# A backward row transform in 64x64 tiles of TensorE, with the halves combined on VectorE

## The chip, the cores and the metric

The kernel runs on one core of one Trainium2 chip. The metric is the device time of one execution in microseconds (us); the median of three executions before the change is 3488.26 us, from 3488.07 to 3488.36. The engines are named PE (TensorE matmul), PEld (TensorE weight load), DVE (VectorE), ACT (ScalarE), POOL (GpSimd) and SP (SyncE, which issues most DMAs).

## The reference

Four layers act on an image batch of 4 x 64 channels x 128 x 128 in fp32: a box convolution, an AFNO block stack, and two more box convolutions. The change touches the AFNO stack alone, and in it only the inverse transform. Cut to what matters, one of its four blocks computes, for each of the four images:

```python
xf = jnp.fft.rfft2(_ln(xp, ln1w, ln1b), axes=(1, 2), norm='ortho')
# ... two 64x64 complex channel mixes (relu, then a threshold mask) per frequency
xs = jnp.fft.irfft2(xc, s=(H, W), axes=(1, 2), norm='ortho')
x = residual + jnp.transpose(xs, (0, 3, 1, 2))
h = jax.nn.gelu(_ln(xp2) @ mw1 + mb1, approximate=False)
x = x + jnp.transpose(h @ mw2 + mb2, (0, 3, 1, 2))
```

irfft2 is done as matrix products: first along the row frequencies (the part that is changed, called backward in the kernel), then along the column frequencies (called inverse).

## The kernel before, in words

Function `afno_layers` works through 16 runs (4 images x 4 blocks), numbered n. A run takes 16 steps q, a step takes 4 slots s. In every step each engine does one sixteenth of the MLP of run n (transpose in, up product, gelu, down product, transpose back, residual add). In between, in the slots, it does parts of the Fourier path of run n+1: forward transform, spectrum (the channel mixes), backward, and the first inverse parts. There is no scheduler: each engine's program is written out in this order, `parts_before` and the constants `U_...` tell which parts fall into which slot, and semaphores tie the engines together. Each engine takes its instructions in order.

Backward stands in step 11, slots 44 to 47. Before the change it is 16 parts, four in a slot. A part is four channels: PE multiplies the masked spectrum of each channel (128 row frequencies x 128) by the matrix `dft_hi` (128 x 128) into one PSUM bank (line 1756), and one copy brings the bank into `iy`, which shares the memory of `g`; VectorE copies the even parts (L1431), ScalarE the odd ones (L1568). Four banks are used in turn, so a part waits only for the copy of the part four earlier. fp32 products appear in the trace as two weight loads and two matmuls each.

Step 11 is one of the steps in the list `CLOSED`: PE does the two transposes (L1792 back, L1786 in), then all of backward without a break, and then the MLP products: up (L1766), down (L1777), up (L1766). Step 12 then begins with inverse part 0 (L1687 to L1691), which waits until all of `iy` is there. In step 11 VectorE also does the residual add (L1437) and two sums over a strip of the image (`sum_up`: L1456 sums the strip, L1459 sums its squares, which ScalarE makes at L1610). In three of the sixteen backward sections (where `fresh(n)` holds and another image is to come) ScalarE also fills a strip of a stage (`fill_stage`, L1621) between the second and the third slot of step 11.

```python
parts(n, q, 0, inverse, forward, spectrum, backward)    # slot 0 of a step
late = (2 if q in CLOSED else 3) if q == 5 or q % 4 == 3 and fresh(n) else 1
```

Of the kernel before, what the change touches and what calls it, by code (L numbers as in the profile page):

```python
# [32 lines left out]
P = 128  # L33
# [27 lines left out]

def constants():
# [10 lines left out]
    out[DFT_HI] = np.cos(turn)  # L73
    out[DFT_HI][:, HALF + 1:] = np.sin(turn[:, HALF + 1:])
# [12 lines left out]
    mirror = np.eye(P)[-n % P]  # L87
    out[SYM_E], out[SYM_O] = (np.eye(P) + mirror) / 2, (np.eye(P) - mirror) / 2
# [798 lines left out]
U_INVERSE, U_FORWARD, U_SPECTRUM, U_BACKWARD, U_NEXT, U_END = 0, 4, 20, 39, 55, 59  # L887
# [7 lines left out]
def parts_before(slot):  # L895
# [7 lines left out]
    if slot <= NEXT_SLOTS[0]:  # L903
        return U_BACKWARD + 4 * (slot - BACKWARD_SLOT)
# [105 lines left out]
def afno_layers(nc, const, w, src, dst, kept, early, s_early, s_early_par, s_last):  # L1010
# [6 lines left out]
    with ExitStack() as ctx:  # L1017
# [14 lines left out]
        bank = [psum(f"bank{i}") for i in range(4)]  # L1032
# [14 lines left out]
        iy = g[:].rearrange("p k r c -> p (k r c)")[:, 0:C * P].rearrange("p (h c) -> p h c", c=C)  # L1047
# [41 lines left out]
        s_ih, s_iy = sem("ih"), [sem("iy_dve"), sem("iy_act")]  # L1089
# [14 lines left out]
        def o1_of(j):  # L1104

            return odd[:].rearrange("p h c -> p (h c)") if j % 2 else o1[:]

# [48 lines left out]
        with nc.Block() as block:  # L1156
# [185 lines left out]
            def _(dve):  # L1342
# [132 lines left out]
                for n, q in periods():  # L1475
# [6 lines left out]
                    if q in CLOSED and 0 <= Q - 2 < BLOCKS * RUNS:  # L1482
                        residual(Q - 2)
                    parts(n, q, 0, inverse, forward, spectrum, backward)
# [15 lines left out]
                    strips = strips_at(n, q)[:1]  # L1500
                    late = (2 if q in CLOSED else 3) if q == 5 or q % 4 == 3 and fresh(n) else 1
                    for s in range(1, 4):
# [4 lines left out]
                        if s == late:  # L1507
# [4 lines left out]
                        if s == late + 1 and q in CLOSED:  # L1512
# [9 lines left out]
            def _(act):  # L1522
# [143 lines left out]
            def _(pe):  # L1666
# [11 lines left out]
                def inverse(n, j):  # L1678
                    if j == 0:
                        pe.wait_ge(s_iy[0], GROUPS // 2 * (n + 1))  # L1680
                        pe.wait_ge(s_iy[1], GROUPS // 2 * (n + 1))
# [67 lines left out]
                def backward(n, i):  # L1749
# [3 lines left out]
                    if i >= 4:  # L1753
# [132 lines left out]
```

## Time and profile before

| what | value |
|---|---|
| median of three executions | 3488.26 us |
| the profiled execution's own time | 3488.49 us |
| its span, first to last instruction | 3486.2 us |
| PE busy | 3236.5 us, 93% |
| DVE / ACT / POOL busy | 2363.6 / 2197.1 / 1689.7 us |
| mean granted TensorE clock | 0.962 |
| PE, backward matmuls (L1756) | 235.7 us busy, 2048 instructions |
| DVE, copies of backward (L1431) | 88.5 us, 128 instructions |
| ACT, copies of backward (L1568) | 76.0 us, 128 instructions |

The time outside the span is 2.3 us. A matmul's end is modelled, and matmuls are pipelined, so the distance from one start to the next says more than a duration. The granted clock is given as a share of 2.4 GHz, whose two levels here are 2.4 and 1.2 GHz.

### The profile page before, as it was taken

What the parts mean: (1) busy time and instruction counts of PE and PEld (TensorE: products, weight loads), DVE (VectorE), ACT (ScalarE), POOL (GpSimd) and SP (SyncE); (2) the same over time, 40 slices, a digit from 0 to 9 for tenths busy, and PEclk for the clock granted to TensorE, in tenths of its full rate; (3) what the DMA queues carried; (4) which work ended last, traced back from release to release, by engine and by line L of the source; (5) the groups of instructions that cost most, each with busy time, mean ns of one, the idle gap of its engine ahead of it and who ended that gap; (6) DMA issues with size and microseconds to landing.
All of it is one profiled execution on the core that took longest, in us unless ns stands there. A gap on an engine that the chain in (4) does not pass through costs nothing. (4 is left out here: it accounts for less than half of the span.)

```text
span 3486.2 us, 52802 instructions
## 1 busy us (share of the span) xinstructions
PE 3236.5 (93%) x18285; PEld 1963.5 (56%) x18285; DVE 2363.6 (68%) x4046; ACT 2197.1 (63%) x3477; POOL 1689.7 (48%) x1421
## 2 busy tenths in 40 slices
PE   6945699999999999999999999999999999979689
PEld 2735465657565656464646565757565656344257
DVE  4956667777777676766666767676767675536667
ACT  3955566666666666767676666575757575646468
POOL 4435546464646455555464655545454643310242
PEclk7967899999999999999999999999999999989789
DMA  9860001010202111313120111111111111457898
GB/s 328 274 200 19 37 31 66 32 67 31 67 31 67 37 66 39 120 43 142 50 88 37 65 41 61 43 55 43 55 43 55 43 55 43 169 178 204 273 292 241
DMA packets 250280, 334.10 MB, mean 96 GB/s; under 512 B 22304, under 2 KB 195616, under 8 KB 242608
## 3 DMA queue, kind: packets, MB, share of 16 engines
q1 hardware_dynamic: 241664, 315.29, 26.8%
q0 software_dynamic: 7904, 15.57, 1.6%
q8 instruction: 145, 2.38, 0.3%
q14 instruction: 103, 0.84, 0.1%
q10 hardware_dynamic: 464, 0.02, 0.0%
HBM read 188.06 MB, written 142.74 MB: 95 GB/s over the span
## 5 line engine op out<-in xcount | busy, mean ns | idle before, releaser
L1576 ACT ACTIVATE images<-a_wide,a_up_b 128x1024 f32<-128x1024 f32 x512 | 569.8, 1113 | 253.0 <-PE a_wide L1766 249.7
L1766 PE MATMUL a_wide<-images 64*128 64x512 f32 x2048 | 579.0, 641 | 26.6 <-ACT images L1576 25.9
L1318 POOL TENSOR_TENSOR images<-a_o,a_mag 128x256 f32<-128x256 f32 (+1 forms) x512 | 360.4, 730 | 371.6 <-DVE a_mag L1426 368.8
L1276 POOL TENSOR_TENSOR images<-images,a_stat 128x512 f32<-128x512 f32 x256 | 267.2, 1044 | 544.6 <-DVEq L1473 528.1
L1777 PE MATMUL a_result<-images 128*64 128x512 f32 x2048 | 495.9, 605 | 1.8 <-DVE images L1437 1.8
L1406 DVE TENSOR_TENSOR a_o<-a_bank,a_mix_b 128x512 f32<-128x512 f32 (+1 forms) x272 | 180.9, 665 | 248.7 <-PE a_bank L1723 241.8
L1739 PEld LDWEIGHTS a_bank<-a_dft_h,a_g 128*128 128x128 f32 x2080 | 272.4, 191 | 129.0 <-issue 129.0
L1766 PEld LDWEIGHTS a_wide<-images 64*128 64x128 f32 x2048 | 156.6, 185 | 289.2 <-issue 259.4
L1437 DVE TENSOR_TENSOR images<-a_result,images 128x512 f32<-128x512 f32 x256 | 175.7, 686 | 205.6 <-PE a_result L1792 205.2
L1777 PEld LDWEIGHTS a_result<-images 128*64 128x64 f32 x2048 | 124.4, 136 | 322.4 <-issue 318.8
L1459 DVE TENSOR_REDUCE a_stat<-a_sq 128x16 f32<-128x1024 f32 x240 | 290.7, 1211 | 22.1 <-ACT a_sq L1610 20.4
L1705 PE MATMUL a_bank<-dft_w,images 128*128 128x128 f32 x2048 | 246.1, 279 | 46.5 <-POOL images L1301 45.2
L1716 PE MATMUL a_bank<-a_xf,a_mix_fold 128*128 128x512 f32 (+1 forms) x544 | 283.2, 602 | 6.0 <-ACT a_xf L1563 6.0
L1456 DVE TENSOR_REDUCE a_stat<-images 128x16 f32<-128x1024 f32 x232 | 281.4, 1213 | 7.2 <-DVE a_stat L1005 0.5
L1705 PEld LDWEIGHTS a_bank<-dft_w,images 128*128 128x128 f32 x2048 | 235.6, 193 | 81.9 <-POOL images L1301 45.3
L1589 ACT ACTIVATE images<-a_result,a_down_b 128x512 f32<-128x512 f32 x256 | 175.5, 685 | 166.5 <-PE a_result L1777 166.5
L1739 PE MATMUL a_bank<-a_dft_h,a_g 128*128 128x128 f32 x2080 | 277.3, 275 | 1.8 <-DVE a_g L1399 1.8
L1610 ACT ACTIVATE a_sq<-images 128x1024 f32<-128x1024 f32 x216 | 226.8, 1050 | 26.1 <-DVE a_stat L1459 25.2
L1756 PE MATMUL a_bank<-a_dft_hi,images 128*128 128x128 f32 x2048 | 235.7, 278 | 5.2 <-POOL images L1318 5.2
L1756 PEld LDWEIGHTS a_bank<-a_dft_hi,images 128*128 128x128 f32 x2048 | 232.7, 194 | 8.6 <-POOL images L1318 8.6
L1264 POOL TENSOR_TENSOR images<-images,a_odd 128x512 f32<-128x512 f32 (+1 forms) x128 | 160.9, 1257 | 103.3 <-DVE images L1373 101.5
L420 ACT ACTIVATE box_pre<-box_bank,box_affine_k 128x128 f32<-128x128 f32 x512 | 192.2, 457 | 26.9 <-PE box_bank L484 25.1
(206 smaller groups left out, 6109.9 us busy)
## 6 DMA issues: line engine op xcount, KB each, us to landing
rows<-images SPq DMA_DIRECT2D x112, 512.0 KB, 2.6
images<-rows SPq DMA_DIRECT2D x105, 512.0 KB, 3.7
box_xc<-in_x SPq DMA_DIRECT2D x16, 1024.0 KB, 16.5
box_x<-in_x SPq DMA_DIRECT2D x64, 256.0 KB, 4.5
turned<-box_o SPq DMA_DIRECT2D x64, 256.0 KB, 3.6
images<-turned SPq DMA_DIRECT2D x16, 1024.0 KB, 13.0
planes<-box_work SPq DMA_DIRECT2D x64, 256.0 KB, 3.5
box_xc<-planes SPq DMA_DIRECT2D x16, 1024.0 KB, 18.8
```

The lines of the kernel that those rows point to most:

```text
L1276: G.tensor_tensor(rows(y2[:, i % 2]), x[:, row:row + HB], r[:, :, None].broadcast_to([P, HB, C]), ALU.mult).then_inc(s_y2, 1)
L1318: ins = G.tensor_tensor(y[n % 2][:, :, to].rearrange("p c k -> p k c"), o2[:, j % 3, lo:4, r], mask[:, lo:4], ALU.mult)
L1456: V.tensor_reduce(to, strip, AX.X, ALU.add)
L1459: V.tensor_reduce(to, squares_of(r, kind, u), AX.X, ALU.add).then_inc(s_sq_read, 1)
L1576: A(hidden[:, i % 2, j], wide[:], ACT.Gelu, bias=up_b2[:, l, j:j + 1]).then_inc(s_hid, 1)
L1610: A(squares_of(r, kind, u), strip, ACT.Square).then_inc(s_sq, 1)
L1705: mm = M(bank[i % 4][:, c * P:(c + 1) * P], y[n % 2][:, 4 * i + c, :], dft_w[:], start=True, stop=True)
L1716: M(bank[2][:, 0:cols], mix1_fold[:, l], xf[:, 0:cols], start=True, stop=True).then_inc(s_mix1, 1)
L1739: mm = M(bank[0][:, k * P:(k + 1) * P], g[:, first_kw(t) + k].rearrange("p r c -> p (r c)"), dft_h[:], start=True, stop=True)
L1756: mm = M(bank[i % 4][:, c * P:(c + 1) * P], y[n % 2][:, 4 * i + c, :], dft_hi[:], start=True, stop=True)
L1766: mm = M(wide[:, half * BANK:(half + 1) * BANK], up_fold[cs, l, j * P:(j + 1) * P], yc[cs, i % 2], start=True, stop=True)
L1777: mm = M(result[half * C:(half + 1) * C, :], down[:, l, j, :], hidden[:, i % 2, j, half * BANK:(half + 1) * BANK], start=j == 0, stop=j == ...
```

## The change

The row frequencies are sorted, even ones in partitions 0 to 63, odd ones in 64 to 127 (`row_frequencies`; `dft_h`, the two mirror matrices and `dft_hi` are permuted to match). For even and for odd frequencies a row transform to 128 points follows from 64 values each. So a channel becomes four products of 64 x 64 by 64 columns, one for each pairing of a half of the frequencies (rows of PE's array and one PSUM bank of a pair) with a half of the columns of the image (columns of the array, partitions 0 to 63 or 64 to 127 of PSUM).

A part is now eight channels, there are 8 parts, two in a slot, and a part takes a pair of banks; there are two pairs. ScalarE copies the end rows and then one half of each bank (512 elements of a partition) to `xf` or `o1`; VectorE adds that half to the other one in PSUM (512 elements), and subtracts it in two more operations (256 and 248 elements). PE may start a part when VectorE is through with the part two earlier. In step 11, where `fresh(n)` doesn't hold, VectorE's sum of the strip moves ahead of the first part and its sum of squares behind the last.

```diff
+def row_frequencies():
+    return np.arange(P).reshape(HALF, 2).T.reshape(-1)
...
-U_INVERSE, U_FORWARD, U_SPECTRUM, U_BACKWARD, U_NEXT, U_END = 0, 4, 20, 39, 55, 59
+U_INVERSE, U_FORWARD, U_SPECTRUM, U_BACKWARD, U_NEXT, U_END = 0, 4, 20, 39, 47, 51
...
-        return U_BACKWARD + 4 * (slot - BACKWARD_SLOT)
+        return U_BACKWARD + 2 * (slot - BACKWARD_SLOT)
...
+        pair = [ctx.enter_context(nc.psum_tensor(f"a_pair{i}", [P, 2 * BANK], F32)) for i in range(2)]
+        bank = [pair[i // 2][:, i % 2 * BANK:(i % 2 + 1) * BANK] for i in range(4)]
...
                 def backward(n, i):                      # VectorE
-                    if i % 2 == 0:
-                        dve.wait_ge(s_ih, GROUPS * n + i + 1)
-                        V.tensor_copy(iy[:, :, 4 * i:4 * i + 4], four(bank[i % 4]).rearrange("p c h -> p h c")
-                                      ).then_inc(s_iy[0], 1)
+                    quarter = HALF // 2
+                    dve.wait_ge(s_ih, C // 8 * n + i + 1)
+                    dve.wait_ge(s_first_half, C // 8 * n + i + 1)
+                    first = first_half_of(i).rearrange("p t c h -> p t h c")
+                    second = of_kh(i)[:, :, :, 0, :].rearrange("p t c h -> p t h c")
+                    V.tensor_tensor(iy_rows(i, 0, [P - quarter + 1, 2], [1, quarter]), first, second[:, ::-1], ALU.add)
+                    V.tensor_tensor(iy_rows(i, HALF, [-1, quarter]), first[:, 0], second[:, 1], ALU.subtract)
+                    V.tensor_tensor(iy_rows(i, P - quarter - 1, [-1, quarter - 1]), first[:, 1, 0:quarter - 1],
+                                    second[:, 0, 0:quarter - 1], ALU.subtract).then_inc(s_iy, 1)
...
+                    around = q == 11 and not fresh(n)
+                    if around:
+                        for strip in strips:
+                            sum_up(*strip, 0)
                     parts(n, q, 0, inverse, forward, spectrum, backward)
...
-                        if s == late:
+                        if s == late and not around:
...
-                        if s == late + 1 and q in CLOSED:
+                        if s == (3 if around else late + 1) and q in CLOSED:
...
                 def backward(n, i):                      # ScalarE
-                    if i % 2 == 1:
-                        act.wait_ge(s_ih, GROUPS * n + i + 1)
-                        A(iy[:, :, 4 * i:4 * i + 4], four(bank[i % 4]).rearrange("p c h -> p h c"), ACT.Copy
-                          ).then_inc(s_iy[1], 1)
+                    quarter = HALF // 2
+                    act.wait_ge(s_ih, C // 8 * n + i + 1)
+                    if i >= 2:
+                        act.wait_ge(s_iy, C // 8 * n + i - 1)
+                    ends_of_kh = bass.AP(pair[i % 2], quarter - 1, [[2 * BANK, P], [BANK + quarter, 2], [HALF, 8]])
+                    A(iy_rows(i, quarter, [HALF, 2]), ends_of_kh, ACT.Copy)
+                    A(first_half_of(i), of_kh(i)[:, :, :, 1, :], ACT.Copy).then_inc(s_first_half, 1)
...
                 def backward(n, i):                      # TensorE
-                    if i >= 4:
-                        pe.wait_ge(s_iy[i % 2], GROUPS // 2 * n + i // 2 - 1)
-                    for c in range(4):
-                        mm = M(bank[i % 4][:, c * P:(c + 1) * P], y[n % 2][:, 4 * i + c, :], dft_hi[:], start=True, stop=True)
+                    if i >= 2:
+                        pe.wait_ge(s_iy, C // 8 * n + i - 1)
+                    for c in range(8):
+                        for part in range(2):
+                            to = slice(part * HALF, (part + 1) * HALF)
+                            for odd_kh in range(2):
+                                kh = slice(odd_kh * HALF, (odd_kh + 1) * HALF)
+                                mm = M(bank[2 * (i % 2) + odd_kh][to, c * HALF:(c + 1) * HALF], y[n % 2][kh, 8 * i + c, to],
+                                       dft_hi[kh, 0:HALF], start=True, stop=True)
                     mm.then_inc(s_ih, 1)
```

On PE the order is the same. This is step 11 and the beginning of step 12 of the seventh image, first before, then after; `a_result` is the PSUM bank of the MLP's down product, `a_wide` that of the up product, `a_pair` are the two bank pairs.

```order
L1792 MATMUL a_result<-ident,images 128x128 x4
L1786 MATMUL a_turned<-ident,images 128x128 x4
L1756 MATMUL a_bank<-a_dft_hi,images 128x128 x64
L1766 MATMUL a_wide<-images 128x512 x2
L1777 MATMUL a_result<-images 64x512 x4
L1766 MATMUL a_wide<-images 128x512 x2
L1687 MATMUL a_bank<-a_g,a_idft_e 128x512
```

```order
L1833 MATMUL a_result<-ident,images 128x128 x4
L1827 MATMUL a_turned<-ident,images 128x128 x4
L1796 MATMUL a_pair<-a_dft_hi,images 64x64 x256
L1807 MATMUL a_wide<-images 128x512 x2
L1818 MATMUL a_result<-images 64x512 x4
L1807 MATMUL a_wide<-images 128x512 x2
L1723 MATMUL a_pair<-a_g,a_idft_e 128x512
```

The 64 products of 128x128 became 256 of 64x64; nothing else on PE moved.

On VectorE in step 11 of the same image, first before, then after (`a_g` is `iy`, `a_stat` takes the sums, `a_xf` and `a_o` are the two buffers of the first half; three of the four rounds of six rows are left out):

```order
L1437 TENSOR_TENSOR images<-a_result,images 128x512
L1431 COPY a_g<-a_bank 128x128x4 x4
L1456 TENSOR_REDUCE a_stat<-images 128x16
L1431 COPY a_g<-a_bank 128x128x4 x2
L1459 TENSOR_REDUCE a_stat<-a_sq 128x16
L1431 COPY a_g<-a_bank 128x128x4 x2
L1372 TENSOR_TENSOR images<-a_bank,images 128x512
```

```order
L1467 TENSOR_TENSOR images<-a_result,images 128x512
L1486 TENSOR_REDUCE a_stat<-images 128x16
L1459 TENSOR_TENSOR a_g<-a_xf,a_pair 128x2x32x8
L1460 TENSOR_TENSOR a_g<-a_xf,a_pair 128x32x8
L1461 TENSOR_TENSOR a_g<-a_xf,a_pair 128x31x8
L1459 TENSOR_TENSOR a_g<-a_o,a_pair 128x2x32x8
L1460 TENSOR_TENSOR a_g<-a_o,a_pair 128x32x8
L1461 TENSOR_TENSOR a_g<-a_o,a_pair 128x31x8
...
L1489 TENSOR_REDUCE a_stat<-a_sq 128x16
L1397 TENSOR_TENSOR images<-a_pair,images 128x512
```

Eight copies became 24 additions and subtractions, and the two sums moved from among them to either side.

## Rows read from the trace of the kernel before

**Rows 1.** The page: busy time and share of each engine; busy tenths in 40 slices.

```profile
PE 3236.5 (93%) x18285; PEld 1963.5 (56%) x18285; DVE 2363.6 (68%) x4046; ACT 2197.1 (63%) x3477; POOL 1689.7 (48%) x1421
...
PE   6945699999999999999999999999999999979689
...
PEclk7967899999999999999999999999999999989789
```

**Rows 2.** Groups by line: forms, count, busy us, mean ns, idle before, releaser.

```profile
L1756 PE MATMUL a_bank<-a_dft_hi,images 128*128 128x128 f32 x2048 | 235.7, 278 | 5.2 <-POOL images L1318 5.2
```

**Rows 3.** Timeline of step 11, seventh image: start us, us, instruction, [idle before].

```profile
1386.89 0.69 DVE L1437 TENSOR_TENSOR images<-a_result,images 128x512 f32<-128x512 f32 x1 [1.63 <-PE a_result L1792]
...
1387.28 14.56 PE L1756 MATMUL a_bank<-a_dft_hi,images 128*128 128x128 f32 x128
...
1388.48 0.69 DVE L1431 COPY a_g<-a_bank 128x512 f32<-128x512 f32 x1 [0.90 <-PE a_bank L1756]
1389.37 0.60 ACT L1568 ACTIVATE a_g<-a_bank 128x512 f32<-128x512 f32 x1 [1.45 <-PE a_bank L1756]
...
1391.65 1.05 ACT L1610 ACTIVATE a_sq<-images 128x1024 f32<-128x1024 f32 x1
...
1394.45 1.21 DVE L1456 TENSOR_REDUCE a_stat<-images 128x16 f32<-128x1024 f32 x1
...
1401.77 1.13 PE L1766 MATMUL a_wide<-images 64*128 64x512 f32 x4
...
1403.31 0.14 PEld L1777 LDWEIGHTS a_result<-images 128*64 128x64 f32 x2 [0.29 <-issue]
1403.74 0.14 PEld L1777 LDWEIGHTS a_result<-images 128*64 128x64 f32 x2 [0.29 <-issue]
```

**Rows 4.** Timeline, PE at the start of step 12.

```profile
1405.76 1.12 PE L1687 MATMUL a_bank<-a_g,a_idft_e 128*128 128x512 f32 x2
```

**Rows 5.** Windows: length, then busy us of each engine, granted clock, DMA share.

```profile
1387.28:1401.77 14.49, 14.49 (x129) 14.37 (x128) 8.02 (x11) 5.77 (x10) 11.25 (x5) 1.00 0.34 110
```

**Rows 6.** Timeline of the later box layer: products in four column tiles.

```profile
3143.03 0.16 PEld L802 LDWEIGHTS box_bank<-box_work,box_w1bd 128*32 128x32 f32 x8 [0.17 <-issue]
3143.03 1.96 PE L802 MATMUL box_bank<-box_work,box_w1bd 128*32 128x512 f32 x15
```

**Rows 7.** Timeline of DVE: two additions of 512 elements, one behind the other.

```profile
2984.30 0.68 DVE L1372 TENSOR_TENSOR images<-a_bank,images 128x512 f32<-128x512 f32 x1
...
2984.90 0.68 DVE L1373 TENSOR_TENSOR images<-a_bank,images 128x512 f32<-128x512 f32 x1
```

**Rows 8.** The same view: two operations of some 256 elements.

```profile
1312.54 0.42 DVE L1130 COPY a_g<-a_bank 64x252 f32<-64x252 f32 x1 [0.23 <-PE a_bank L1705]
1312.88 0.42 DVE L1391 TENSOR_SCALAR a_g<-a_bank 64x260 f32<-64x260 f32 x1
```

**Rows 9.** Groups by line: the shortest operation of ACT on PSUM.

```profile
L1554 ACT ACTIVATE a_odd<-a_bank,a_mix_b 128x1 f32<-128x1 f32 x16 | 4.1, 254 | 1.2 <-PE a_bank L1716 1.2
```

**Rows 10.** Timeline: PE waits for ACT and goes on.

```profile
2975.22 1.11 ACT L1576 ACTIVATE images<-a_wide,a_up_b 128x1024 f32<-128x1024 f32 x1 [0.30 <-PE a_wide L1766]
...
2976.44 0.33 PEld L1766 LDWEIGHTS a_wide<-images 64*128 64x128 f32 x4 [0.49 <-issue]
```

**Rows 11.** Timeline of ACT in a section with the stage fill.

```profile
1570.31 2.00 ACT L1621 ACTIVATE a_stage<-images 128x1024 f32<-128x1024 f32 x1
...
1572.35 1.06 ACT L1610 ACTIVATE a_sq<-a_stage 128x1024 f32<-128x1024 f32 x1
```

**Rows 12.** Windows, as rows 5: two pairs of stretches that follow on each other.

```profile
1635.20:1638.60 3.40, 1.59 (x9) 0.59 (x8) 1.97 (x2) 3.37 (x4) 3.40 (x3) 1.00 0.38 135
1638.60:1642.00 3.40, 3.40 (x11) 2.26 (x10) 1.06 (x2) 2.20 (x3) 3.40 (x3) 0.50 0.92 327
1788.80:1792.20 3.40, 1.63 (x10) 1.32 (x11) 3.28 (x4) 3.19 (x6) 3.40 (x3) 1.00 0.76 243
1792.20:1795.60 3.40, 3.40 (x13) 0.97 (x13) 2.73 (x4) 2.75 (x4) 0.94 (x1) 1.00 0.54 219
```

More of the change, by code:

```diff
@@ L72, in constants @@
     out[DFT_H][HALF + 1:] = -np.sin(turn[HALF + 1:])
-    out[DFT_HI] = np.cos(turn)
-    out[DFT_HI][:, HALF + 1:] = np.sin(turn[:, HALF + 1:])
+    kh = row_frequencies()
+    out[DFT_H] = out[DFT_H][:, kh]
+    quarter = HALF // 2
+    even, odd, low, mid = kh[:HALF], kh[HALF:], n[:quarter], np.arange(P - quarter + 1, P + 1)
+    out[DFT_HI][:HALF, 0:HALF] = np.hstack([np.sin(turn[even][:, mid % P]), np.cos(turn[even][:, low])])
+    out[DFT_HI][:HALF, quarter - 1] = np.cos(turn[even, quarter])
+    out[DFT_HI][HALF:, 0:HALF] = np.hstack([np.cos(turn[odd][:, low]), np.sin(turn[odd][:, mid % P])])
+    out[DFT_HI][HALF:, HALF - 1] = np.sin(turn[odd, P - quarter])
     out[DFT_W][:, :KW] = np.cos(turn[:, :KW]) / P
@@ L87, in constants @@
     mirror = np.eye(P)[-n % P]
+    mirror = mirror[kh][:, kh]
     out[SYM_E], out[SYM_O] = (np.eye(P) + mirror) / 2, (np.eye(P) - mirror) / 2
@@ L1031, in afno_layers @@
         turned, result = psum("turned"), psum("result")
-        bank = [psum(f"bank{i}") for i in range(4)]
+        pair = [ctx.enter_context(nc.psum_tensor(f"a_pair{i}", [P, 2 * BANK], F32)) for i in range(2)]
+        bank = [pair[i // 2][:, i % 2 * BANK:(i % 2 + 1) * BANK] for i in range(4)]
         images = kept["images"]
@@ L1046, in afno_layers @@
         g = sb("g", [P, KW, 2, C])
-        iy = g[:].rearrange("p k r c -> p (k r c)")[:, 0:C * P].rearrange("p (h c) -> p h c", c=C)
+        iy = g[:].rearrange("p k r c -> p (k r) c")
         hidden = third(2 * HC * 2 * BANK).rearrange("p (r j q) -> p r j q", r=2, j=HC)
@@ L1088, in afno_layers @@
         s_top, s_masked, s_sym, s_ends = (sem(n) for n in ("top", "masked", "sym", "ends"))
-        s_ih, s_iy = sem("ih"), [sem("iy_dve"), sem("iy_act")]
+        s_ih, s_first_half, s_iy = sem("ih"), sem("first_half"), sem("iy")
         s_iw, s_odd, s_even, s_x, s_x_up = (sem(n) for n in ("iw", "odd", "even", "x", "x_up"))
@@ L1106, in o1_of, with first_half_of, iy_rows, of_kh @@
             return odd[:].rearrange("p h c -> p (h c)") if j % 2 else o1[:]
+        def first_half_of(i):
+            return (o1 if i % 2 else xf)[:].rearrange("p (t c h) -> p t c h", t=2, c=8)
+        def iy_rows(i, start, *steps):
+            return bass.AP(iy.tensor, start * C + 8 * i, [[2 * KW * C, P], *([step * C, count] for step, count in steps), [1, 8]])
+        def of_kh(i):
+            return pair[i % 2][:].rearrange("p (k c t h) -> p k c t h", k=2, c=8, t=2)
         def mask_of(j):
@@ L1499, in _ @@
                             sum_up(*strip, 1)
-                    strips = strips_at(n, q)[:1]
                     late = (2 if q in CLOSED else 3) if q == 5 or q % 4 == 3 and fresh(n) else 1
@@ L1679, in inverse @@
                     if j == 0:
-                        pe.wait_ge(s_iy[0], GROUPS // 2 * (n + 1))
-                        pe.wait_ge(s_iy[1], GROUPS // 2 * (n + 1))
+                        pe.wait_ge(s_iy, C // 8 * (n + 1))
                     elif j >= 2:
```

2 lines of the change are left out of this document (added).

## The prediction

> **What bounds the kernel now.** I read the page first: PE is busy 93% of the span, in nearly every slice of the AFNO stack 9 tenths or more, at full clock [rows 1]. The chain that ended last only covers the last layer, so it says nothing here. Next the groups by line: backward is 2048 PE instructions in 235.7 us [rows 2], 128 of them in each of 16 sections. Then the timeline of one section: PE starts backward at 1387.28 and its next product at 1401.77, 14.49 us later [rows 3], the same in 14 of the 16 sections within 0.1 us (the first, partly at the low clock, took some 3 us more, the last 0.1 less). In this stretch PE and its weight loads are busy throughout, DVE 8.02 us, ACT 5.77, POOL 11.25 [rows 5]. So here PE alone sets the time, and whatever a section gets shorter or longer, the kernel does too, as long as nobody behind it is late. The question is what will set the length of a section once PE's part shrinks.
>
> **PE's part.** One instruction for 128 columns took 0.112 us (14.49 less 0.1 for the change of tiling at its end, over 128 [rows 3]). Instructions for 512 columns step by 0.43 us (1403.31 to 1403.74) [rows 3]. The line through both gives 0.059 us for 64 columns. A part of 8 channels has 8 x 4 products, each of two instructions. If the four tiles run side by side, the length is 8 x 2 x 0.059 = 0.94 us. All eight parts: 7.6 us, about half of 14.49. Without any overlap it is 3.8 us a part. No row shows 64x64 tiles, so how four of them share the array is the largest unknown. The nearest rows: products of 512 columns in four column tiles took 1.96 us for 15 of them where one alone steps by 0.43 (6.4 us in a row), and their eight weight loads lay within 0.16 us [rows 6]. At least 15 instructions with their loads thus share the array by four, and the steps between loads of different tiles are about 0.01 us. I take four side by side, 0.94.
>
> **The new ring.** Only two bank pairs are left, so PE may start part i when DVE has finished part i-2. One round, from rows:
> - PE's part 0.94.
> - PE to its reader 0.30: a section's first copy starts at 1388.48, 1.20 after PE's start, and four channels take 8 x 0.112 = 0.90 [rows 3].
> - ACT 0.78: the copy of 512 elements 0.60 [rows 3], and ahead of it the end rows. Their nearest row is 254 ns for one element [rows 9]; the next operation starts some 0.07 before its end, so 0.18.
> - ACT to DVE 0.10, from the row where PE goes on 0.11 after ACT's end (2975.22 + 1.11, then 2976.44) [rows 10].
> - DVE 1.37: an addition of 512 elements is followed after 0.60 [rows 7], one of some 256 after 0.34, and the last takes 0.42 [rows 8].
> - DVE back to PE 0.10.
>
> Together 3.59 us for two parts, 1.8 a part, against DVE's own 1.3 and PE's 0.94. So neither engine but the ring sets the pace, and PE waits for half the time. Part 6 starts after 3 rounds, 10.77; part 7 one DVE turn (1.30) later at 12.07 and is through at 13.01. For the changes of tiling on the way in and out I add 0.1 each: the MLP's three products behind the section have eight steps of 0.43, 3.44 us, and take 3.99 (1401.77 to 1405.76 [rows 3, 4]), which leaves under 0.2 for each of three changes. A section becomes 13.2 us, 1.3 less than 14.49.
>
> **What lies beside.** ACT's square (1.05 us at 1391.65 [rows 3]) now stands behind part 1, where ACT is idle until part 2 comes. The moved sum, 1.21 us [rows 3], now begins when the residual add ends (1386.89 + 0.69) and is through at +1.5 us, ahead of the first half's arrival at +2.1. It costs nothing, and if that cover failed at most 0.6 us a section. The sum of squares behind part 7 delays nobody in step 11. Behind ACT's waits stands the next gelu: ACT is through with part 7 at 14.1 us, the up product that the gelu needs ends at 14.3. `iy` is whole at about 15.5 us after the section's start. PE wants it after the MLP's products, which take 4.0 us (1401.77 to 1405.76 [rows 3, 4]), at 17.2, so inverse part 0 has 1.7 us to spare. The permuted constants cost nothing. POOL and SP have the same instructions in the same order, and POOL's 11.25 us [rows 5] fit into 13.2 + 4.0.
>
> **The sections with a stage fill.** In three of the 16 ACT spends 3.0 us between parts 3 and 4 (1570.31 to 1572.35 + 1.06) [rows 11]. Before, four banks hid that. Now ACT's part 4 comes 1.5 us late, which the ring hands on: these sections take 14.6, no gain, a loss of 0.1 each. If the fill fell outside, they would gain 1.3 as well.
>
> **The sum.** 13 x 1.3 less 3 x 0.1 is 16.6 us. From the profiled execution's own 3488.49 that gives 3471.9; it is 0.23 above the median of the runs, so I forecast 3471.7 us, 0.5% faster. Half of what PE's shorter products offer (16 x 6.9 = 110 us) and more goes into the ring. The bounds of the terms: every hand-off 0.05 shorter and the end rows free gives a section of 12.5, minus 28 us in all; VectorE's operations 0.1 us dearer each, since they read with steps that no row shows, gives 14.4, and no gain. The forecast's own range is 3450 to 3480.
>
> **Rivals.**
> 1. No change that can be measured (within 0.2%, 7 us, which is about what a measurement of this kernel can tell from none). The ring is 0.3 us or more a round longer than summed: the three operations with their strides, two waits ahead of the first, and the hand-offs. For it: four of the six terms are not seen in these shapes. Against it: the copy with an output step of 64 elements costs 0.69, the same as plain additions of 512 (0.68) [rows 3, 7]. Section 14.4, gain 0 to 1: 3487.
> 2. Slower, by tiles that share the array by two only, or by starts that can't follow closely enough. Then a part takes 8 x 4 x 0.059 = 1.89 us, the round 4.54, and part 7 ends at 3 x 4.54 + 1.89 + 1.89 + 0.2 = 17.6. That is 3.1 more than now, 50 us in 16 sections: 3538. It is slower as soon as a part takes over 1.25 us. For it: row pairs and column pairs are each seen alone, never together. Against it: rows 6.
> 3. Slower, by the clock. PE now works without a gap in this section; after the change it waits for nearly half of it. The rows show one case each: after a stretch with PE busy 1.59 of 3.40 us the next had a clock of 0.50, and after one with 1.63 of 3.40 it stayed at 1.00 [rows 12]. At 1.2 GHz a part takes 1.88, so the section again takes 17.6, and as the low stretch of 3.4 us in rows 12 reaches into dense work, another 1.7 is lost. 16 x 4.8 = 77 us: 3565. Against it: 0.94 of every 1.8 us is more than 1.59 of 3.40, before the tail of each product is counted.
> 4. Faster still. The fixed hand-offs overlap better than they add up, and DVE sets the pace: part 7 starts after DVE's sixth turn, 2.1 + 6 x 1.3 = 9.9, the section is 11.1, and 16 x 3.4 = 54 us are gained: 3434. For it speaks little; every hand-off in the ring is a wait of another engine.
>
> **The numbers.** Forecast 0.50, rival 1 0.18, rival 2 0.14, rival 3 0.11, rival 4 0.07. Faster is the forecast and rival 4: 0.57. Same 0.18, slower 0.25. The range takes in rival 1, reaches to rival 2's time, and below to halfway between the forecast and rival 4: 3448 to 3538. It leaves out rival 3, most of rival 4 and the worst of rival 2.
>
> **What would show it.** In the changed profile: a section of 13.2 us from the first product of backward to the up product; 16 matmuls of each tile stepping by 0.06 us, so a part that is started within 0.94; PE idle seven tenths of a microsecond or so ahead of each part from the third on, released by VectorE's third operation; ACT's first half 0.60 and DVE's three operations 0.69, 0.43, 0.42; three sections of 14.6 with the fill; a clock of 1.00 throughout; no new wait ahead of inverse part 0. PE's busy sum falls by some 100 us, most of it as new idle time. I am wrong if a part takes over 1.25 us on PE, if the clock falls inside the sections, or if VectorE's operations read PSUM across two banks at another price than these rows.

## The result, and the profile after

The changed kernel takes 3530.03 us (median of 4 runs, 3528.75 to 3532.13), beside 3488.31 us for the kernel before on the same chip. The ratio is 1.012 (95% interval 1.010 to 1.014), 41.7 us slower. The forecast was 3471.7 and faster. The time lies inside the range, but the direction is wrong.

The page of the kernel after (busy us of each engine, then the granted clock in 40 slices) answers to [rows 1]:

```profile
PE 3178.0 (90%) x24429; PEld 1892.0 (54%) x24429; DVE 2540.5 (72%) x4302; ACT 2207.1 (63%) x3605; POOL 1690.5 (48%) x1421
...
PEclk8968899999999999999999999999999999989789
```

PE has 58.5 us less to do and DVE 177 us more. The groups by line say where from (count, then busy us, mean ns, then idle before with its releaser):

```profile
L1796 PE MATMUL a_pair<-a_dft_hi,images 64*64 64x64 f32 x8192 | 177.4, 250 | 96.8 <-DVE a_g L1461 91.3 <-POOL images L1343 4.9
...
L1459 DVE TENSOR_TENSOR a_g<-a_xf,a_pair 128x512 f32<-128x512 f32 x64 | 67.7, 1058 | 27.5 <-ACT a_xf L1606 25.7
...
L1460 DVE TENSOR_TENSOR a_g<-a_xf,a_pair 128x256 f32<-128x256 f32 x64 | 38.0, 594 | 0.0
...
L1606 ACT ACTIVATE a_xf<-a_pair 128x512 f32<-128x512 f32 x64 | 37.9, 592 | 0.0
...
L1461 DVE TENSOR_TENSOR a_g<-a_xf,a_pair 128x248 f32<-128x248 f32 x64 | 37.2, 581 | 0.0
```

VectorE's three operations take 1.06, 0.59 and 0.58 us. I had taken 0.69, 0.43 and 0.42, from [rows 7, 8]. ScalarE's copy is as forecast. PE waits 91.3 us for VectorE's third operation.

A section is the time from the first product of backward to PE's next product. This is the second of the 16 sections, at full clock, shown as [rows 3] is (start us, us, instruction, idle before it):

```profile
541.82 2.10 PE L1796 MATMUL a_pair<-a_dft_hi,images 64*64 64x64 f32 x128
...
543.04 0.18 ACT L1605 ACTIVATE a_g<-a_pair 128x16 f32<-128x16 f32 x1 [0.58 <-PE a_pair L1796]
543.12 0.59 ACT L1606 ACTIVATE a_xf<-a_pair 128x512 f32<-128x512 f32 x1
543.82 1.05 DVE L1459 TENSOR_TENSOR a_g<-a_xf,a_pair 128x512 f32<-128x512 f32 x1 [0.45 <-ACT a_xf L1606]
543.98 0.18 ACT L1605 ACTIVATE a_g<-a_pair 128x16 f32<-128x16 f32 x1 [0.26 <-PE a_pair L1796]
...
544.78 0.61 DVE L1460 TENSOR_TENSOR a_g<-a_xf,a_pair 128x256 f32<-128x256 f32 x1
545.31 0.57 DVE L1461 TENSOR_TENSOR a_g<-a_xf,a_pair 128x248 f32<-128x248 f32 x1
545.81 1.07 DVE L1459 TENSOR_TENSOR a_g<-a_o,a_pair 128x512 f32<-128x512 f32 x1
...
545.94 1.16 PE L1796 MATMUL a_pair<-a_dft_hi,images 64*64 64x64 f32 x64 [2.03 <-DVE a_g L1461]
...
556.18 1.16 PE L1796 MATMUL a_pair<-a_dft_hi,images 64*64 64x64 f32 x64 [0.82 <-DVE a_g L1461]
...
557.28 1.13 PE L1807 MATMUL a_wide<-images 64*128 64x512 f32 x4
```

Read it from the first DVE operation. It starts 2.00 us after PE, and from there VectorE hardly stops (three waits of 0.04 to 0.07 us): one part after the other at some 2.06 us, until PE gets part 7 after six turns, at 2.00 + 6 x 2.06 = 14.36 (556.18). The section ends at 15.46 (to 557.28). PE streams 0.93 of every 2.06 us.

In most sections something else comes on top. The same view of the seventh section (the one called the seventh image so far; the batch has four images, and each of the 16 runs has one section):

```profile
1405.72 1.79 PE L1796 MATMUL a_pair<-a_dft_hi,images 64*64 64x64 f32 x64 [0.85 <-DVE a_g L1461]
...
1407.84 1.86 PE L1796 MATMUL a_pair<-a_dft_hi,images 64*64 64x64 f32 x64 [0.33 <-DVE a_g L1461]
...
1408.33 1.07 DVE L1459 TENSOR_TENSOR a_g<-a_o,a_pair 128x512 f32<-128x512 f32 x1 [0.54 <-ACT a_o L1606]
...
1410.45 1.16 PE L1796 MATMUL a_pair<-a_dft_hi,images 64*64 64x64 f32 x64 [0.76 <-DVE a_g L1461]
...
1416.41 1.13 PE L1807 MATMUL a_wide<-images 64*128 64x512 f32 x4
```

The windows of both sections (length, busy us of PE, PEld, DVE, ACT, POOL, granted clock, DMA share, GB/s), which answer to [rows 5]:

```profile
541.81:557.28 15.47, 9.01 (x514) 8.11 (x513) 14.82 (x22) 6.30 (x17) 11.35 (x5) 1.00 0.33 106
1399.57:1416.41 16.84, 11.76 (x514) 10.77 (x513) 14.82 (x22) 6.29 (x17) 11.33 (x5) 0.80 0.30 97
```

The mean granted clock is 0.80 in this section, so part of it ran at 1.2 GHz. There a part takes some 1.8 us instead of 1.16 (from first start to modelled end), so VectorE now waits (the 0.54), and the section is 1.4 us longer. The clock falls in 11 of the 15 sections behind the first, for 3.4 to 10.2 us each.

**Where the 40 us are.** I measure from the first backward product to the first inverse product and call this the stretch, since the MLP between them is the same. Before, it is 18.47 us (14.49 + 3.98) in every section behind the first (18.37 in the last). After, it is 19.45 or so at full clock (four sections), 19.97 to 21.09 in nine sections with a low clock, and 23.09 and 22.90 in the two with the stage fill; over sections 2 to 16 the sum goes from 277.0 to 311.0 us. Of these 34.0, 15 x 0.98 = 14.7 is VectorE's pace alone, 12.3 the low clock in the nine, 7.1 the two fill sections beyond 19.45 (all rounded). From the first section's start to the second's another 5.0 us are lost, with 26.7 us of it at the low clock where there were 19.6. Together 39.0 of the 40.3 that the span grew.

### The profile page after: what moved, and what is told of

Same layout as the page of the kernel before. It is cut to its first block and busy times, and to the rows that moved or that the text cites. A ratio compares the mean times of both kernels' runs of the same rounds, so it can differ in the third digit from the quotient of the medians.

```text
span 3526.5 us, 65682 instructions
## 1 busy us (share of the span) xinstructions
PE 3178.0 (90%) x24429; PEld 1892.0 (54%) x24429; DVE 2540.5 (72%) x4302; ACT 2207.1 (63%) x3605; POOL 1690.5 (48%) x1421
## 5 line engine op out<-in xcount | busy, mean ns | idle before, releaser
L1431 DVE TENSOR_TENSOR a_o<-a_pair,a_mix_b 128x512 f32<-128x512 f32 (+1 forms) x272 | 181.1, 666 | 248.5 <-PE a_pair L1759 241.7
L1775 PEld LDWEIGHTS a_pair<-a_dft_h,a_g 128*128 128x128 f32 x2080 | 272.4, 191 | 129.0 <-issue 129.0
L1489 DVE TENSOR_REDUCE a_stat<-a_sq 128x16 f32<-128x1024 f32 x240 | 291.0, 1212 | 22.5 <-ACT a_sq L1647 20.8
L1741 PE MATMUL a_pair<-dft_w,images 128*128 128x128 f32 x2048 | 246.5, 279 | 47.7 <-POOL images L1326 45.2
L1752 PE MATMUL a_pair<-a_xf,a_mix_fold 128*128 128x512 f32 (+1 forms) x544 | 283.2, 602 | 6.0 <-ACT a_xf L1597 5.9
L1741 PEld LDWEIGHTS a_pair<-dft_w,images 128*128 128x128 f32 x2048 | 235.9, 193 | 83.3 <-POOL images L1326 45.3
L1775 PE MATMUL a_pair<-a_dft_h,a_g 128*128 128x128 f32 x2080 | 277.3, 275 | 1.8 <-DVE a_g L1424 1.8
L1796 PE MATMUL a_pair<-a_dft_hi,images 64*64 64x64 f32 x8192 | 177.4, 250 | 96.8 <-DVE a_g L1461 91.3
L1796 PEld LDWEIGHTS a_pair<-a_dft_hi,images 64*64 64x64 f32 x8192 | 160.5, 161 | 115.0 <-DVE a_g L1461 106.4
```

The costliest lines, as they stand in the source:

```text
L1489: V.tensor_reduce(to, squares_of(r, kind, u), AX.X, ALU.add).then_inc(s_sq_read, 1)
L1741: mm = M(bank[i % 4][:, c * P:(c + 1) * P], y[n % 2][:, 4 * i + c, :], dft_w[:], start=True, stop=True)
L1752: M(bank[2][:, 0:cols], mix1_fold[:, l], xf[:, 0:cols], start=True, stop=True).then_inc(s_mix1, 1)
L1775: mm = M(bank[0][:, k * P:(k + 1) * P], g[:, first_kw(t) + k].rearrange("p r c -> p (r c)"), dft_h[:], start=True, stop=True)
L1796: mm = M(bank[2 * (i % 2) + odd_kh][to, c * HALF:(c + 1) * HALF], y[n % 2][kh, 8 * i + c, to], dft_hi[kh, 0:HALF], start=True, stop=True)
```

## The experiments

Theory S: VectorE's operations are dear because they read the first half in SBUF with a step of 32 elements from one element to the next. Theory P: it is the PSUM operand, read with a step of 64 elements across two banks. Theory C: the loss is the clock's.

**e1: the first half laid out in the order in which VectorE reads it.** ScalarE's copy then writes with a step.

```diff
-            return (o1 if i % 2 else xf)[:].rearrange("p (t c h) -> p t c h", t=2, c=8)
+            return (o1 if i % 2 else xf)[:].rearrange("p (t h c) -> p t c h", t=2, c=8)
```

> Only the buffer of the first half changes its layout: ScalarE writes it as (t h c), so that VectorE reads it in runs of 8 channels side by side, no longer with a step of 32 elements. In the changed kernel VectorE's three operations take 1.06, 0.60 and 0.58 us where 0.69, 0.43 and 0.42 were summed. Theory S (the step in the SBUF operand is what costs): they fall to 0.69, 0.43, 0.42, ScalarE's copy stays at 0.59, the section falls from 15.46 us (at full clock) to about 13.3 and the time to about 3480 or below, with fewer clock falls. Rival P (the step of 64 elements in the PSUM operand): the operations stay at 1.06, 0.60, 0.58 and the time at 3530. Rival D (the output in runs of 8 elements, 256 B apart): likewise unchanged.

3506.23 us, ratio 1.0038 (1.0024 to 1.0052), against 3491.69 before on that chip. Groups by line:

```profile
L1606 ACT ACTIVATE a_xf<-a_pair 128x512 f32<-128x512 f32 x64 | 71.1, 1111 | 0.0
...
L1459 DVE TENSOR_TENSOR a_g<-a_xf,a_pair 128x512 f32<-128x512 f32 x64 | 44.0, 688 | 87.0 <-ACT a_xf L1606 66.9 <-PE a_pair L1796 20.1
...
L1460 DVE TENSOR_TENSOR a_g<-a_xf,a_pair 128x256 f32<-128x256 f32 x64 | 26.4, 413 | 0.0
```

VectorE is back at the prices of [rows 7, 8], with its output in the same order as before: theory S holds, and rival D, the output's order, falls. The step has moved to ScalarE's write, whose copy went from 592 to 1111 ns, and so into the ring. I had expected that copy to stay at 0.59 us, and so the time was not 3480.

**e2: the PSUM operand in order instead.** The matmul writes eight channels side by side, with a step of 8.

```diff
-            return pair[i % 2][:].rearrange("p (k c t h) -> p k c t h", k=2, c=8, t=2)
+            return pair[i % 2][:].rearrange("p (k t h c) -> p k c t h", k=2, c=8, t=2)
...
-                                mm = M(bank[2 * (i % 2) + odd_kh][to, c * HALF:(c + 1) * HALF], y[n % 2][kh, 8 * i + c, to],
+                                mm = M(bank[2 * (i % 2) + odd_kh][to].rearrange("p (f c) -> p f c", c=8)[:, :, c], y[n % 2][kh, 8 * i + c, to],
```

> Only the layout in PSUM changes: TensorE writes the 64 results of a channel with a step of 8, so that ScalarE and VectorE read runs of 8 channels. The buffer of the first half in SBUF keeps its step of 32 elements. Theory S: VectorE's operations stay at 1.06, 0.60, 0.58 us and the time at 3530. Rival P: they fall to 0.69, 0.43, 0.42 and the time to about 3480. Rival D: unchanged, 3530. If TensorE's writes with a step cost something, its part grows beyond 0.93 us.

3532.13 us, ratio 1.0119 (1.0102 to 1.0136), as after:

```profile
L1459 DVE TENSOR_TENSOR a_g<-a_xf,a_pair 128x512 f32<-128x512 f32 x64 | 67.5, 1055 | 28.3 <-ACT a_xf L1606 26.9
...
L1460 DVE TENSOR_TENSOR a_g<-a_xf,a_pair 128x256 f32<-128x256 f32 x64 | 37.9, 592 | 0.0
```

Theory P falls. A part of PE's still takes 0.93 us, although its writes now have a step. The same view shows ScalarE's copy at 592 ns with either PSUM layout.

**e3: both layouts.**

> Both layouts as in the two runs before. If one operand's step alone costs, this equals the better one of the two, about 3480. If both have to go (the operation runs at the pace of its worst operand), only this one has 0.69, 0.43, 0.42 us and a section of 13.3 us at full clock. Rival D (output runs): still 1.06, 0.60, 0.58 and about 3530. On the clock: with a ring of 1.8 us a part TensorE streams 0.93 of it instead of 0.93 of 2.06; if low stretches remain, sections of 15 to 16 us remain among those of 13.3.

3504.07 us, ratio 1.0035 (1.0024 to 1.0046), VectorE 687/413/404 ns and ScalarE 1110: as e1, and not the 3480 that I expected, for the same reason. ScalarE reads PSUM with a step of 8 in e2 and in e3; only e3 also writes SBUF with one, and only there the copy is dear. So it is the write.

**e4: surplus products in PE's gaps, to keep the clock.** The rest is the kernel after. The products go to a bank that nobody reads then.

```diff
+                    if 2 <= i < 8 and 0 <= n - 1:
+                        if i == 2:
+                            pe.wait_ge(s_yc, BLOCKS * (n - 1) + 13)
+                        for c in range(8 if i == 2 else 4):
+                            M(turned[:, c % 4 * P:(c % 4 + 1) * P], dft_hi[:], dft_hi[:], start=True, stop=True)
```

> The changed kernel with surplus matmuls (128x128, result unused, into the idle bank of the transposes) ahead of TensorE's wait in parts 2 to 7 of backward, 0.9 us of them a part (1.8 ahead of part 2), which fit into the idle 1.1 us (2.0 us). VectorE's work is untouched. Theory: of the 41.7 us lost, 14 to 17 come from VectorE's longer turn (1.0 us a section at full clock) and the rest, some 25 us, from low stretches of TensorE's clock inside and behind the sections. Then no section shows a low clock, all are 15.5 us but for the three with a fill (15.5 to 17), and the time is about 3505. Rival (the low clock costs nothing, the sections are long for another reason, such as VectorE being disturbed): the clock stays at 1.00 and the time at 3530. Rival (surplus work delays TensorE): over 3530.

3531.21 us, ratio 1.0114 (1.0098 to 1.0131). None of the sections 2 to 16, which are those with filler, has a low clock any more. But the filler and its changes of tiling took 1.2 us a part, so PE itself stepped by 2.18 and the stretches became 20.2 to 21.5 us. It doesn't price the clock.

**e6: the same with 6 and 2 products.**

> The changed kernel with less surplus work in TensorE's gaps than before: two 128x128 products a part (six ahead of part 2), results unused. With four of them no stretch had a low clock, but the surplus and the changes of tiling took longer than VectorE's turn (TensorE stepped by 2.18 us a part), and the sections were 16.5 us. Two take 0.45 us and the two changes 0.3, which with 0.93 is under 2.06. Theory (clock): no low stretch in the sections, 15.5 us each, 16.9 at most with a stage fill, time about 3508 on a chip where the kernel before takes 3491.7. Rival (the low clock costs nothing that counts): 3530 as without the surplus.

3522.06 us, ratio 1.0095 (1.0080 to 1.0110), 8 us below after and not the 22 that I expected. No low clock in sections 2 to 16, stretches of 19.5 to 20.9 us, their sum 300.5 instead of 311.0. Here are the fill section 8 and the second section, which answer to [rows 5]:

```profile
1576.86:1593.75 16.89, 13.74 (x545) 12.12 (x544) 13.70 (x21) 8.20 (x18) 11.37 (x5) 1.00 0.35 128
542.89:558.46 15.57, 13.73 (x545) 12.12 (x544) 14.97 (x22) 6.30 (x17) 11.37 (x5) 1.00 0.32 105
```

So of the 34 us at least 10.5 are the clock's (the filler still costs something, and PE stops in the middle of a part eight times here, on which more at e5), and most of the rest stays: theory C is a part and not the cause. The 14.7 us stand without it. In the two fill sections the stretch is 20.88 and 20.92 us, where after has 23.09 and 22.90.

**e5: the layout of e1, and ScalarE goes through the copy in the same order,** so that no SBUF operand has a step.

```diff
-                    A(first_half_of(i), of_kh(i)[:, :, :, 1, :], ACT.Copy).then_inc(s_first_half, 1)
+                    A(first_half_of(i).rearrange("p t c h -> p t h c"),
+                      of_kh(i)[:, :, :, 1, :].rearrange("p t c h -> p t h c"), ACT.Copy).then_inc(s_first_half, 1)
```

> The buffer of the first half as in the first of the earlier experiments (channels side by side), and ScalarE now goes through it in the same order, channels innermost, so that it writes runs of 8 to SBUF and takes the step of 64 elements in PSUM. There VectorE's operations fell to 0.69, 0.41 and 0.40 us, but ScalarE's copy rose from 0.59 to 1.11. Theory (an access to SBUF with a step of 32 bytes or more between elements costs about double, a step in PSUM nothing, on both engines): now both are short, 0.59 and 0.69, 0.41, 0.40; a section at full clock takes 13.2 us, as was forecast, and the time lies at 3475 to 3490, depending on how many sections have a low clock. Rival (ScalarE pays for any order that differs from PSUM's own): its copy stays at 1.1 and the time at 3505.

3483.14 us (11 runs), ratio 0.9985 (0.9976 to 0.9994): 47 us below after, a little faster than before, and inside the 3475 to 3490 that I expected. Groups, then a section of this kernel:

```profile
L1459 DVE TENSOR_TENSOR a_g<-a_xf,a_pair 128x512 f32<-128x512 f32 x64 | 44.0, 687 | 73.4 <-ACT a_xf L1606 73.4
...
L1606 ACT ACTIVATE a_xf<-a_pair 128x512 f32<-128x512 f32 x64 | 37.9, 592 | 0.0
...
L1797 PE MATMUL a_pair<-a_dft_hi,images 64*64 64x64 f32 x8192 | 153.7, 227 | 76.6 <-DVE a_g L1461 60.2 <-issue 10.4 <-POOL images L1343 4.9
```

```profile
877.68 2.10 PE L1797 MATMUL a_pair<-a_dft_hi,images 64*64 64x64 f32 x128
...
881.08 2.41 PE L1797 MATMUL a_pair<-a_dft_hi,images 64*64 64x64 f32 x128 [1.31 <-DVE a_g L1461]
...
884.48 0.91 PE L1797 MATMUL a_pair<-a_dft_hi,images 64*64 64x64 f32 x43 [0.99 <-DVE a_g L1461]
...
885.72 1.50 PE L1797 MATMUL a_pair<-a_dft_hi,images 64*64 64x64 f32 x85 [0.33 <-issue]
```

The ring is 3.40 us for two parts (881.08 to 884.48), and this section is 13.17 us. Both engines read PSUM with a step of 64 elements and pay nothing for it. New is the row marked issue: PE stops in the middle of a part, with nothing to wait for. Measured from the start of one product to the start of the next, there are 22 such stops of 0.3 to 1.6 us, 15.7 us in all, and none in the kernel after.

**e7 and e8: does it help to let the MLP's work of step 11 into the slots?** e7 is e5 with step 11 out of `CLOSED` and the sums back among the slots; e8 the kernel before with step 11 out.

```diff
-CLOSED = (0, 1, 7, 8, 9, 11)
+CLOSED = (0, 1, 7, 8, 9)
```

> As the run with both readers in order, and in addition step 11 is no longer in the list CLOSED: TensorE does the up product of the MLP after the second slot and the down product after the third instead of both behind all of backward, ScalarE its gelu and its delta likewise, and VectorE its sums after the second slot. Theory: TensorE's gaps of some 0.8 us a part are filled with work that is due anyway, up to 3 us a section, so 13.2 us of backward and 4.0 of MLP overlap, and the low clock is gone: 16 x (1.3 + 2 to 3) under the kernel before, some 3430 to 3450. Rival (the gelus and sums now stand in the ring of ScalarE and VectorE and lengthen it by as much): no better than the closed step, about 3480.

> Control: the kernel before with step 11 opened in the same way and nothing else. There TensorE has no gap in backward, so there is nothing to fill: within 0.3% of the kernel before if the opened step alone brings nothing; if it gains, that part of the gain of the opened changed kernel is not due to the gaps.

e7: 3482.74 us, ratio 0.9978 (0.9969 to 0.9987), the stretch 17.76 us. e8: 3494.41, ratio 1.0014 (1.0004 to 1.0023), 18.86. So e7 is where e5 is (3483.14), and my theory of 3430 to 3450 fails; the rival's 3480 came, although only one of the sections 2 to 16 has a low clock and PE stops in the middle of a part twice. What the interleaving saves on PE goes back into a longer ring: two parts take 4.76 to 4.95 us in e7 and 3.40 at best in e5. The edit puts gelu and sums among the parts together, so which of them lengthens it stays open.

**e9: e5 with the MLP's products placed one by one.** In step 11 the up product goes ahead of part 2, the down products ahead of parts 4 and 6, ScalarE's gelu behind part 3's copy; the edits for ScalarE's gelu and for splitting the down product are left out below. VectorE's order is that of after. **e10** is the same without the layout of e5, **e11** the same order in the kernel before.

```diff
+                    if q == 11 and 0 <= Q < BLOCKS * RUNS:
+                        mlp_up(Q, 1)
...
+                        if q == 11:
+                            if s < 3 and 0 <= Q - 1 < BLOCKS * RUNS:
+                                mlp_down(Q - 1, [s - 1])
+                            continue
```

> The kernel after, its first half of a part stored in the order in which VectorE reads it and written so by ScalarE (as in e5), and with the MLP's products of step 11 taken into the gaps between parts: the up product ahead of part 2, the first down product ahead of part 4, the second ahead of part 6; ScalarE's gelu stands behind part 3's copy. PE's work from the start of backward to the first inverse product is then 8 parts x 0.93 + 1.06 + 2 x 0.93 = 10.4 us plus the third down product (0.9) and some changes of tiling; VectorE's ring of 8 x about 1.35 + 2.1 + the residual of the MLP sets some 13.5 to 15.5. Theory (VectorE's price mended, the ring leaves PE gaps that due work can fill): 15 to 16.5 us instead of 18.47 before, no low clock in the section, period per run 167 to 168, time 3445 to 3460. Rival (PE's products are late or hold back the ring, or TensorE outruns its instruction loading again): the stretch 17.5 or more, several stalls per section marked issue, time 3480 or above.

> The kernel after with VectorE's dear reads left as they are (1.06 + 0.60 + 0.58 a part) and the MLP's products of step 11 taken into the gaps between parts as in e9. Theory (VectorE sets the pace at about 2.06 us a part, and the clock falls since PE only streams 0.93 of it): with products in three of the gaps the clock falls in fewer sections; from the start of backward to the first inverse product 8 x 1.9 + about 2 = 17 to 18 us, against 19.4 in sections of after at full clock and 21 at the low one; time 3495 to 3515. Rival (the low clock costs nothing of its own, since VectorE sets the pace either way, and the work in the gaps delays the ring): 19.4 or more, time 3525 to 3540.

> Control: the kernel before with the same MLP products of step 11 at the same places between parts. In the kernel before PE has no gaps in this section, so the same work in another order takes the same time, plus four more changes of tiling. From the start of backward to the first inverse product 18.5 to 19.2 us (18.47 before), time 3488 to 3500, ratio 1.000 to 1.003. If the order by itself were what e9 gains, this would be faster than 3480.

| kernel | us | ratio to before (95%) | stretch, most sections |
|---|---|---|---|
| e9 | 3462.43 | 0.9925 (0.9911 to 0.9938) | 15.7 to 16.6 us |
| e10 | 3515.95 | 1.0077 (1.0062 to 1.0093) | 18.52 to 18.86 |
| e11 | 3498.56 | 1.0026 (1.0015 to 1.0037) | 19.21 |

The stretch is longer in the fill sections (17.54 and 18.55 us in e9, 22.41 and 21.70 in e10) and in one more of e10 (19.92). e9 beats both kernels, 28 us below before and 2 above the range that I expected. Its PE in the sixth section:

```profile
1209.20 2.10 PE L1797 MATMUL a_pair<-a_dft_hi,images 64*64 64x64 f32 x128
...
1211.23 1.13 PE L1808 MATMUL a_wide<-images 64*128 64x512 f32 x4
...
1212.60 2.41 PE L1797 MATMUL a_pair<-a_dft_hi,images 64*64 64x64 f32 x128 [0.24 <-DVE a_g L1461]
...
1214.94 1.08 PE L1820 MATMUL a_result<-images 128*64 128x512 f32 x4
...
1217.20 1.62 PE L1797 MATMUL a_pair<-a_dft_hi,images 64*64 64x64 f32 x95 [0.24 <-issue]
...
1224.92 1.13 PE L1724 MATMUL a_pair<-a_g,a_idft_e 128*128 128x512 f32 x2 [1.33 <-DVE a_g L1461]
```

The wait of 1.31 us ahead of part 2 in e5 is 0.24 here. The stretch, 15.72 us, ends with a wait for VectorE again. (The third down product of my expectation does not exist; the trace has two.) Low clock is in one of the sections 2 to 16, a stage fill one. The order by itself isn't what wins: e11 is slower than before, as its stretch of 19.21 (18.47) says. With VectorE's dear reads, e10 stays 53.5 us above e9. But it is 14 us below after: its stretch is 18.52 where after's at full clock is 19.45, and 3 of its sections 2 to 16 have a noticeable low stretch instead of 11. That is 1 us above the time and 0.5 above the stretch that I expected, and the rival's 3525 falls.

**e12: the moved sums put back.**

```diff
-                    around = q == 11 and not fresh(n)
+                    around = False
```

> The kernel after with one part of the change undone: in step 11 the sums of the strips stand where they stood in the kernel before. Theory (the moved sum is hidden beside the first parts, and VectorE's three operations alone set the pace): the same time as after within 0.2%, 3525 to 3535; put back inside VectorE's turns it may cost up to 16 x 0.6 = 10 us, 3540. Rival (the moved sums are part of the loss, since they delay the first turn): 3520 or less.

3552.61 us, ratio 1.0180 (1.0164 to 1.0196): 22.6 us above after, twice what I expected at most. VectorE in one section:

```profile
2131.35 0.57 DVE L1461 TENSOR_TENSOR a_g<-a_o,a_pair 128x248 f32<-128x248 f32 x1
2131.84 1.20 DVE L1486 TENSOR_REDUCE a_stat<-images 128x16 f32<-128x1024 f32 x1
2132.97 1.01 DVE L1459 TENSOR_TENSOR a_g<-a_xf,a_pair 128x512 f32<-128x512 f32 x1
```

The sum takes 1.13 us from the engine that sets the pace. The one stretch without a low clock is 20.33 (19.45 after). The edit acts in the 12 sections where `fresh(n)` doesn't hold, so this is 12 x 0.88 = 10.6 us. In these 12 the sum of the stretches grew by 22.5 us. The rest goes with a clock that is low more often: PE waits longer, and 14 of the sections 2 to 16 have 3.4 to 13.7 us of it, where 11 had 3.4 to 10.2. So the second part of the change, moving the sums, is a gain within the new form.

## Why the prediction was wrong

**The failed step is VectorE's term of the ring.** I took 1.37 us from [rows 7, 8]. It measured 2.06. The other terms held or came out smaller, in the section at 541.8: PE's part 0.93 (between ACT's two starts, 543.04 and 543.98; forecast 0.94), PE to ACT 0.30 (0.30), ACT 0.67 (0.78), ACT to DVE 0.11 (0.10), DVE to PE 0.06 (0.10). The round is 4.13 us instead of 3.59, and just as long as two of VectorE's turns. So the two ways of reckoning, ring and VectorE-bound, fall together: my fourth rival's sum, 2.1 + 6 turns, gives 14.46 with the true turn, and part 7 started at 14.36. A section at full clock is 15.46 us where I had summed 13.2. Rival 1 had the right cause, the operations with their strides, at too small a size.

I had named this bound ("0.1 us dearer each ... gives 14.4, and no gain"), but 0.1 was no bound, the excess being 0.37, 0.17 and 0.16. The error lies in the argument against rival 1, that a copy with a step costs the same as plain additions [rows 3, 7]. The step from element to element in that copy is in PSUM, where e2 and e5 show it to be free; to SBUF it writes runs of four channels. The changed operation has its step in an SBUF source, and none of the rows that I took shows one. I asked about the engine's step and not about the memory. Among my signs of being wrong stood VectorE's operations at another price for reading PSUM across two banks: the right operations, and the wrong operand.

The Trainium skill has a price for the nearest case, in Vector Engine (DVE) Microarchitecture Reference, section 5.2, Measured stream behaviour on trn2: one source in SBUF that hops by 4 KiB at every 4-byte element costs 1.73 ns an element instead of 1.05. The same table has 2.50 ns for two sources that step by 24 words, and no row for one source with this case's step of 32 words. The trace agrees with the first: (1058 - 688) / 512 = 0.72 ns more. An estimate by that row is (512 + 256 + 248) x 0.68 = 0.69 us more a part, which is what I missed (2.06 - 1.37).

**Rival 3, the clock, is part of it, as a follow-up.** The clock fell in 11 of 15 sections, where PE streams 0.93 of 2.06 us. With VectorE at its forecast price (e5, 0.93 of 1.70) only 3 of the 15 have a low stretch. It was priced at 4.8 us a section, as if PE's slower part set the pace. It cost 0.5 to 1.6 in the nine sections without a fill, because VectorE's 2.06 us cover most of a part of 1.8.

**Rival 2 falls.** The four tiles do run side by side: 64 matmuls in 0.93 us, 14.6 ns each on average. The floor of 25 ns from start to start that I cited from the Trainium skill (TensorE: Matmul & The Clock Gate) does not hold across tiles here.

**The fill sections** were to be 14.6 us, 1.4 more than the others. After has 18.2 and 18.4 (the third is the first section, which is partly at the low clock before and after). ScalarE comes to part 4 late as forecast, behind the fill, but it adds to a longer ring, and the clock falls while PE waits. The fill's own price was about right: without a low clock these sections take 16.9 us in e6, where most others take 15.5 to 16.0, and 14.0 and 14.4 in e5. So at least some 1.3 and 1.5 us of the 18.2 and 18.4 are the clock's.

**The moved sums** cost nothing, as forecast: in the section at 541.8 VectorE was through with its sum 0.45 us before it could start part 0. What they save I had not forecast: 22.6 us by e12.

**With VectorE's term mended** (e5) a section is 13.17 at best, forecast 13.2. That is two errors that cancel: the round is 3.40 instead of 3.59, and a stop inside a part takes 0.55, from start to start. Over the kernel e5 gains 6.6 us and not 16.6. What the sections show for the difference are the stops (15.7 us in all, partly beside the ring's waits) and the low stretches in three sections; no run takes them apart.

**Slips in the sums.** Every hand-off 0.05 us shorter and the end rows free take 0.33 off each of three rounds, so that bound is a section of 12.2 and not 12.5. Halfway between the forecast and rival 4 is 3453, not the 3448 at which the range ends. The estimate by the 25 ns floor is, by the ring's own sum, a section of some 16.1 us and not 15.6. None of the three changes the direction.

**What stays open:** what causes PE's stops inside a part, and what decides in which sections the clock falls.

## What to carry to other kernels

Before you price an operation by a row with "the same" shape, compare for each operand the memory it is in and the distance between elements that follow on each other: an SBUF operand with a step here cost both the reader (VectorE) and the writer (ScalarE), a PSUM operand did not. When two engines hand data over through SBUF, let both walk it in memory order and put the transposition on the PSUM side. When PE's part of a ring shrinks, fill its gaps with products that are due. The mended operations took 47 us off the kernel after and so only made up for its loss; the products placed between parts took another 21 (e9 against e5), and 14 even with the dear reads (e10 against after). The kernel before, which has no gaps there, got slower by the same order (e11).

## What the runs showed of the hardware

- A step between elements in SBUF: VectorE, one of two sources with a step of 32 fp32 elements, 1058 against 688 ns for 512 elements. ScalarE, writing with a step of 8, 1111 against 592 ns. A step of 64 elements in PSUM, either engine: nothing. A matmul writing PSUM with a step of 8 (e2): a part still takes 0.93 us.
- Four 64x64 tiles of fp32: 64 matmuls of 64 columns in 0.93 us, with their 64 loads.
- PE's stops: the kernel after has 24,429 matmuls where there were 18,285, and the instruction queue moves 193 packets of 16 KB where it moved 145. That is 12,288 more instructions of PE (each matmul has a weight load) in 48 more packets, 256 to a packet. In e5 and e9, where PE waits least, it stops 22 and 23 times in the middle of a part for 15.7 and 15.3 us in all. Each stop begins 0.8 to 2.9 us after such a packet set off and ends 2.2 to 3.4 us after that. Where several of them fall into one section of e5, they stand 128 matmuls apart, which is again 256 instructions: in the sixth section after 170, 298 and 426 of its 512 products. That PE outruns the loading of its instructions fits all of this, but no run took the loading away, so it is not shown. The page Runtime: NRT & Kernel Launch of the Trainium skill, section Instruction fetch mechanics, says that this loading is hidden by a floor of some 20 cycles an instruction in the pace of issue. The trace shows 128 instructions in 0.93 us, 7.3 ns each, so it is doubtful that such a floor hides it here.
- The clock: where PE worked 0.93 of every 2.06 us it was granted 1.2 GHz for a while in 11 of 15 sections and 2.4 GHz throughout in the four others, with the same code. It was granted 1.2 GHz in 3 of 15 with 0.93 of every 1.70 us (e5) or with three products in the gaps (e10), and in none with filler in them (e4, e6).
